# Front of a six-layer transformer kernel on one core: five small inputs moved to ScalarE's queue, context sums on two engines, value products issued later, products nobody reads put into waits

## The reference, cut to what matters

```python
x = x + L0_xattn(layernorm(x), ctx)     # x @ W1.T + mean over the 1601 context rows @ W2.T + b
x = x + L0_attn(layernorm(x))           # 16 heads of 16, scores + slopes[h] * (k - q), softmax
x = x + L0_ffn(layernorm(x))            # routed experts and a shared gated MLP (sw1, sw3, sw2)
x = x + L1_xattn(layernorm(x), ctx)     # 16 heads over 1601 keys and values made from ctx
x = x + L1_attn(layernorm(x))           # causal convolution, gated recurrence, gated MLP
x = x + L1_ffn(layernorm(x))            # 256 to 1024 to 256, quantized
```

## Time and profile before

| what | us |
|---|---|
| median of 3 runs | 2172.41 (2168.35 to 2173.95) |
| the profiled execution's own time | 2174.97 |
| its span in the profile | 2173.2 |
| TensorE busy | 1977.2 (91% of the span) |
| VectorE, ScalarE, GpSimd busy | 1328.9, 1049.6, 613.0 |

### The profile page before, as it was taken

One profiled execution on the slowest core, in us unless ns is written; L12 is line 12 of the kernel. 1 busy time (PEld: TensorE's weight loads), 2 busy tenths in 40 slices (PEclk: granted clock), 3 DMA queues, 4 the chain that ended last, 5 costly groups with the idle time before them and its releaser, 6 DMA issues.

```text
span 2173.2 us, 72578 instructions
## 1 busy us (share of the span) xinstructions
PE 1977.2 (91%) x31813; PEld 1596.8 (73%) x31813; DVE 1328.9 (61%) x2495; ACT 1049.6 (48%) x1534; POOL 613.0 (28%) x998
## 2 busy tenths in 40 slices
PE   4788989999999999999999999999999988999887
PEld 4567777777877777777777777777777777777764
DVE  2456755856666567656656676665666666565534
ACT  2344545554455555545555555554544444434432
POOL 3222332323233232333323223332323222122201
PEclk8899999999999999999999999999999999999999
DMA  4343423433423343334233424243342321222122
GB/s 160 140 150 109 142 87 125 149 125 124 139 88 114 116 141 129 130 107 151 83 125 109 171 77 138 92 150 106 110 148 89 116 79 31 89 83 81 48 66 72
DMA packets 99255, 243.91 MB, mean 112 GB/s; under 512 B 13312, under 2 KB 19584, under 8 KB 98944
## 3 DMA queue, kind: packets, MB, share of 16 engines
q1 hardware_dynamic: 98944, 239.26, 32.5%
HBM read 235.94 MB, written 3.15 MB: 110 GB/s over the span
## 4 chain that ended last, share of the span: by engine, by line
PE 71%; DVE 14%; ACT 9%; issue 4%; SPq 1%; POOL 1%; DMA 1%; DVEq 0%; POOLq 0%; ACTq 0%
PE M L780 12%; PE SC L977 9%; PE M L787 9%; PE SC L1000 8%; PE O L1021 7%; ACT probT L1220 6%; PE X L827 5%; DVE mx L1559 4%; PE SC L993 3%; PE M L827 3%; PE X L1101 2%; PE M L868 2%; DVE oT L1571 1%; PE X L1088 1%; PE M L832 1%
## 5 line engine op out<-in xcount | busy, mean ns | idle before, releaser
L1559 DVE TENSOR_REDUCE mx<-SC 128x4 f32<-128x1600 f32 (+1 forms) x256 | 466.5, 1822 | 131.4 <-PE SC L977 128.2
L1220 ACT ACTIVATE probT<-SC 128x2048 f32<-128x2048 f32 (+1 forms) x256 | 398.8, 1558 | 227.2 <-PE SC L1000 226.5
L634 POOL TENSOR_TENSOR rowsT<-raw,rowsT 128x384 fp32r<-128x384 f32 (+1 forms) x256 | 277.8, 1106 | 405.0 <-ACT rowsT L1278 404.9
L787 PE MATMUL M<-wvs,rowsT 128*128 128x256 f32 x2496 | 358.3, 292 | 3.2 <-issue 1.6
L780 PE MATMUL M<-rowsT,wks 128*128 128x400 f32 (+1 forms) x1536 | 334.5, 363 | 12.0 <-DVE V L1362 7.6
L780 PEld LDWEIGHTS M<-rowsT,wks 128*128 128x128 f32 x1536 | 276.2, 192 | 84.5 <-issue 61.5
L1362 DVE TENSOR_TENSOR V<-M,bv 128x256 f32<-128x256 f32 (+1 forms) x448 | 159.6, 398 | 287.4 <-PE M L787 276.6
L787 PEld LDWEIGHTS M<-wvs,rowsT 128*128 128x128 f32 x2496 | 314.8, 192 | 23.5 <-issue 3.5
L1165 ACT ACTIVATE kT<-M,bk 128x400 f32<-128x400 f32 (+1 forms) x256 | 151.6, 594 | 350.6 <-PE M L780 350.2
L977 PE MATMUL SC<-kT,bdq 32*128 32x400 f32 (+1 forms) x2048 | 248.1, 553 | 49.9 <-ACT probT L1220 42.7
L1021 PEld LDWEIGHTS O<-probT,V 128*17 128x17 f32 x13312 | 191.3, 98 | 72.2 <-issue 66.6
(11 more groups left out here) (266 smaller groups left out, 2464.1 us busy)
## 6 DMA issues: line engine op xcount, KB each, us to landing
ring<-in_ws_dram SPq DMA_DIRECT2D x428, 256.0 KB, 4.5
raw<-in_ctx_dram SPq DMA_DIRECT2D x32, 1601.0 KB, 8.4
summed<-in_ctx_dram SPq DMA_DIRECT2D x60, 800.5 KB, 4.5
ring<-rounded_scratch SPq DMA_DIRECT2D x64, 256.0 KB, 5.4
out_dram<-x SPq DMA_DIRECT2D x16, 128.0 KB, 3.2
kT<-in_ctx_dram SPq DMA_DIRECT2D x2, 800.5 KB, 8.9
x<-in_x_dram SPq DMA_DIRECT2D x11, 128.0 KB, 2.0
rounded_scratch<-wround SPq DMA_DIRECT2D x8, 128.0 KB, 2.2
```

The lines of the kernel that those rows point to most:

```text
L634: pool.tensor_tensor(rowsT[1][:, c, at], raw[:, c, at], rowsT[0][:, c, at], ALU.subtract).then_inc(low_ready, 1)
L787: mm = pe.matmul(bank[:, (t - 2 * a) * D:(t - 2 * a + 1) * D], rowsT[xp][:, cc, t * P:(t + 1) * P], wvs[wp][:, cc, :], start=(at == cc == ...
L1220: act.activation(probT[step % 3][0:w, :, 0:len(ts), :].rearrange("p j t q -> p j (t q)"), SC[0:w, :, 0:len(ts) * P], ACT.Exp)\
L1559: dve.tensor_reduce(mx[c][:, :, n], SC[:, :, 0:KCH[n][1]], AX.X, ALU.max).then_inc(max_used, 1)
```

## The change

- SP's list: wk and wv come right after the weight ring, on a semaphore of their own (wkv_in); bv0, bo0 and wg follow alone on early_in; bq0, bk0, dist and the two slopes go to ACT's queue, issued first of all there (prep_in). ACT also loads its table for Exp at the start.
- DVE runs prepare() at g = -21, ahead of the sum of raw, and adds up the second half of batch 1's context (kT[1]) itself; ACT adds up the first half only, and does so after its drain of turn1.
- High parts 0 and 1 move to g = -24 on ACT, parts 2 and 3 to -19 and -18; POOL's low parts go to -18, -18, -16 and -13. The weights' high parts go to the end of g = -19 and the low ones to -18. POOL's clear() goes to the first cycle.
- EARLY: the first six key pieces are at -17, -16 and -15, two values at -12, a key at -9 and -8, and a value in each cycle from -7 to -3.
- warm(16) ahead of the first xa, and warm(2) ahead of four of the first maxima steps: products of 512 columns into bank X which nobody reads.
- At the end: IDLE of xq is 15 in place of 5, and busy_rows goes.

The diff, with its unchanged lines cut:

```diff
@@ -92,7 +92,7 @@
-IDLE = {'sums': 2, 'out': 9, 'conv_in': 4, 'pw': 10, 'gru_in': 7, 'hg0': 2, 'hg1': 3, 'gow': 10, 'ff_in': 7, 'ff0': 2, 'fow': 0, 'xq': 5, 'up0': 0, 'hq': 14, 'down': 4}
+IDLE = {'sums': 2, 'out': 9, 'conv_in': 4, 'pw': 10, 'gru_in': 7, 'hg0': 2, 'hg1': 3, 'gow': 10, 'ff_in': 7, 'ff0': 2, 'fow': 0, 'xq': 15, 'up0': 0, 'hq': 14, 'down': 4}
@@ -146,9 +146,12 @@
-EARLY = {-16: [key(0, 0), key(0, 1)], -15: [key(0, 2), key(0, 3)], -14: [value(0), value(1), value(2)], -13: [value(3), value(4)], -12: [value(5)], -11: [key(1, 0)], -10: [key(1, 1)], -9: [key(1, 2)], -8: [key(1, 3)], -3: [value(6)]}
+EARLY = {-17: [key(0, 0), key(0, 1)], -16: [key(1, 0), key(1, 1)], -15: [key(0, 2), key(1, 2)], -12: [value(0), value(1)], -9: [key(0, 3)], -8: [key(1, 3)], -7: [value(2)], -6: [value(3)], -5: [value(4)], -4: [value(5)], -3: [value(6)]}
+
+FIRST_WARM = (1, 2, 3, 4)
 OWN = value(4), value(5), value(6)
-FIRST_SPLITS = (-19, -18, -17, -16)
+
+FIRST_SPLITS = (-24, -24, -19, -18), (-18, -18, -16, -13)
@@ -304,7 +307,7 @@
     yield n + 1, piece
-if g == FIRST_SPLITS[piece]:
+if STEPS * b + k == FIRST_SPLITS[late][piece]:
@@ -468,6 +471,7 @@
                         "O0_ready", "th0_ready", "first_kept", "l0_done"))
+wkv_in, prep_in = sp.sem("wkv_in"), sp.sem("prep_in")
@@ -552,19 +556,13 @@
     issued += 1
-for t, src in ((bv0, d["l0bv"].partition_broadcast(P)), (bo0, d["l0bo"].partition_broadcast(P)), (wg, d["l0wg"]),
-               (bq0, d["l0bq"]), (bk0, d["l0bk"]), (dist, d["dist"])):
+for t, src in ((wk, d["wkv"][:, 0, :, :]), (wv, d["wkv"][:, 1, :, :])):
+    sync.dma_start(t, src).then_inc(wkv_in, 16)
+for t, src in ((bv0, d["l0bv"].partition_broadcast(P)), (bo0, d["l0bo"].partition_broadcast(P)), (wg, d["l0wg"])):
     whole(t, src, early_in)
-head_pairs = d["slopes"].rearrange("(j a) -> a j", a=2)
-for n in range(2):
-    sync.dma_start(slopes[n * S:(n + 1) * S, :], head_pairs[n].partition_broadcast(S),
-                   allow_slow_non_contiguous=True).then_inc(early_in, 16)
-for t, src in ((wk, d["wkv"][:, 0, :, :]), (wv, d["wkv"][:, 1, :, :])):
-    sync.dma_start(t, src).then_inc(in_, 16)
-for t, src in ((bk, d["l1bk"]), (perm, d["perm"]), (bq, d["l1bq"])):
+sync.dma_start(bvv[:, :, :].rearrange("p h f -> p (h f)"), d["l1bv"].partition_broadcast(P)).then_inc(in_, 16)
+for t, src in ((bk, d["l1bk"]), (bq, d["l1bq"]), (bo, d["l1bo"].partition_broadcast(P)), (perm, d["perm"])):
     whole(t, src, in_)
-sync.dma_start(bvv[:, :, :].rearrange("p h f -> p (h f)"), d["l1bv"].partition_broadcast(P)).then_inc(in_, 16)
-whole(bo, d["l1bo"].partition_broadcast(P), in_)
@@ -730,14 +728,14 @@
     split_max(b + 1, 0)
-if g == L0_START[0] + 5:
+if g == L0_START[0] + 4:
...
     if t == 0 and k == 0:
-        pool.wait_ge(in_, 112)
+        pool.wait_ge(in_, 80)
@@ -747,9 +745,9 @@
     if (i, q) == (0, 3):
-        pool.wait_ge(early_in, 128)
+        pool.wait_ge(early_in, 48)
     layer0(i, q)
-if g == L0_START[0] + 1:
+if g == FIRST_CYCLE:
@@ -833,6 +831,9 @@
 def layer0(what, i, kind, f, bank):
+    if (i, kind) == (0, "l0_xa"):
+        pe.wait_ge(cleared, 1)
+        warm(16)
@@ -904,7 +905,7 @@
 if i == 0:
-    pe.wait_ge(early_in, 128)
+    pe.wait_ge(early_in, 48)
@@ -959,12 +960,20 @@
+                def warm(count):
+
+                    for _ in range(count):
+                        pe.matmul(X.rearrange("p (a t) -> p a t", a=4), identb[:, :], identb[:, :].unsqueeze(1).to_broadcast([P, 4, P]),
+                                  start=True, stop=True, skip_group_check=True)
...
                     k0, kn = KCH[n]
+                    if s in FIRST_WARM:
+                        warm(2)
@@ -1036,23 +1045,11 @@
-                def busy_rows(columns_):
-
-                    for wp, xp in PARTS:
-                        for j in range(4):
-                            r = slice(32 * j, 32 * j + 32)
-                            pe.matmul(SC[:, j, 0:columns_], rowsT[wp][r, 0, 0:P], rowsT[xp][r, 1, 0:columns_], start=True, stop=True, skip_group_check=True)
...
                         busy(IDLE.get(kind, 0))
-                        if kind == "xq":
-                            busy_rows(400)
-                            busy_rows(400)
-                            busy_rows(128)
-                            busy_rows(128)
@@ -1115,10 +1112,6 @@
 for b, k in SLOTS:
-    if STEPS * b + k == min(EARLY):
-        pe.wait_ge(in_, 112)
-        pe.wait_ge(cleared, 1)
-        pe.wait_ge(split_ready, 2)
@@ -1136,6 +1129,8 @@
     fill_x(what, b)
+if STEPS * b + k == min(EARLY):
+    pe.wait_ge(split_ready, 2)
@@ -1143,6 +1138,14 @@
+
+                for t, src in ((bq0, d["l0bq"]), (bk0, d["l0bk"]), (dist, d["dist"])):
+                    act.dma_start(full(t), src).then_inc(prep_in, 16)
+                head_pairs = d["slopes"].rearrange("(j a) -> a j", a=2)
+                for n in range(2):
+                    act.dma_start(slopes[n * S:(n + 1) * S, :], head_pairs[n].partition_broadcast(S),
+                                  allow_slow_non_contiguous=True).then_inc(prep_in, 16)
+                act.preload_act_table(ACT.Exp)
@@ -1162,6 +1165,8 @@
 k0, kn = KCH[a]
+if what == (0, *key(0, 0)):
+    act.wait_ge(in_, 80)
@@ -1278,7 +1283,7 @@
 def high_weights():
-    act.wait_ge(in_, 112)
+    act.wait_ge(wkv_in, 32)
@@ -1290,7 +1295,9 @@
                         src = summed[:, :]
-                    act.activation(src, src, ACT.Copy, accum_out=msum[:, j % 2, c:c + 1]).then_inc(sum_added, 1)
+
+                    if (j, c) != (1, 1):
+                        act.activation(src, src, ACT.Copy, accum_out=msum[:, j % 2, c:c + 1]).then_inc(sum_added, 1)
@@ -1307,8 +1314,6 @@
 load_table(b, k, ACT.Gelu)
-if STEPS * b + k == L0_START[0] + 5:
-    high_weights()
@@ -1323,12 +1328,18 @@
 for j, c in sums(b, k):
-    context_sum(j, c)
+    if j > 1:
+        context_sum(j, c)
...
         drain(what)
+for j, c in sums(b, k):
+    if j == 1:
+        context_sum(j, c)
+if STEPS * b + k == L0_START[0] + 3:
+    high_weights()
@@ -1355,6 +1366,8 @@
 m = min(2 * a + 2, KT) - 2 * a
+if what == (0, *value(0)):
+    dve.wait_ge(in_, 80)
@@ -1398,6 +1411,8 @@
 wait_filled(dve, what)
+if i == 0:
+    dve.wait_ge(early_in, 48)
@@ -1717,7 +1732,7 @@
 def prepare():
-    dve.wait_ge(early_in, 128)
+    dve.wait_ge(prep_in, 80)
@@ -1731,7 +1746,7 @@
 def clear():
-    dve.wait_ge(in_, 112)
+    dve.wait_ge(in_, 80)
@@ -1744,10 +1759,11 @@
 if (i, q) == (0, 1):
+    prepare()
...
     dve.tensor_reduce(msum[:, 0, :], raw[:, :, 0:KEYS], AX.X, ALU.add).then_inc(fast_sum, 1)
-if (i, q) == (0, 3):
-    prepare()
+    dve.wait_ge(batch_landed, 32)
+    dve.tensor_reduce(msum[:, 1, 1:2], kT[1][:, 0:KEYS], AX.X, ALU.add).then_inc(sum_added, 1)
```

## The result

| | before | after |
|---|---|---|
| median, 11 runs each on one chip | 2173.95 (2168.35 to 2180.63) | 2185.26 (2179.32 to 2204.4) |
| ratio, with its 95% interval | | 1.0062 (1.0038 to 1.0087) |
| the profiled execution's own time | 2174.97 | 2184.64 |
| its span | 2173.2 | 2182.8 |
| TensorE busy | 1977.2 | 1977.6 |

The change is slower by over 0.3%. The profiled pair is 9.7 us apart, and it splits so: 1.8 us of it lie ahead of the first exponential of the batches, 7.8 lie between the first and the last of their 256 exponentials, and none behind. (The last row is worked out from the starts of the exponentials of the scores, L1225 in after and L1220 in before, as the traces have them.) TensorE is busy for the same time in both: what was lost is idle time.

A forecast was written before the change was run, and what follows sets the result against it. TensorE, busy 1733 of 1850 us at 2.4 GHz from 200 to 2050, was taken as the bound, so only front and end could move: +1.2 + 1.8 - 3.9 + 1.1 - 1.2 = -1.0 us off 2172.41, 2171.4, range 2161 to 2181.

The forecast's parts named there:

- the side that had 0.21: Chance given to slower by over 0.3%: 0.18 for late slopes, 0.03 for pt0 to sw2 giving nothing with late slopes.
- 1, xa: Front, up to the first xa: DVE does prepare and two sums after the slopes land; start at 22.7, 4.6 us later.
- T: Time when the last of the two slopes' transfers lands, on ACT's queue: taken as 13.0 us, ends 11.5 and 22.
- 2, xa to strips: Front, first xa to the strips: qk's drain no longer waits for prepare, 3.4 us less, 13.6 in place of 17.0.
- 3, strips to pt0: Front, strips to pt0: four keys now stand on PE ahead of ACT's exponential; 17.1 us, 1.8 more.
- 4, pt0 to sw2: Front, pt0 to sw2: value pieces and keys leave PE, at most 8.4 us won; 3.9 less taken, ends 0 and 8.4.
- 5, sw2 to the first maxima: Front, sw2 to the first maxima step: a value piece now stands on PE before the first queries' product; 1.1 us more.
- 6, maxima steps, and on to the first exponential: Six maxima steps: value pieces keep PE busy, three steps run at the higher clock; 1.2 us less.
- 7, the end: Kernel's end: 15 unread products finish about when the old ones did and the last xq waits for DVE; nothing either way.
- any change between 200 and 2050 us: Listed sign that the prediction is wrong: the long middle stretch, taken as unchanged, moves at all.
- third rival: Front: slopes share the engines with big transfers and land near 20; with 22, xa 9 us later, 2180.4 us; chance 0.18.
- second rival: Maxima steps and first scores: value pieces and unread products hold 2.4 GHz there; 2165 us; chance 0.14.

The follow-up runs named there:

- e5: The kernel before with 12 small unread float products (48 TensorE instructions) in the wait for the first xa: 2189.40 us, ratio 1.0080.
- e3: The changed kernel with prepare() on DVE put back behind the sums, at step q = 3: 2180.62 us, ratio 1.0017 to the kernel before.
- e7: The changed kernel without the 24 unread products of its front: 2179.62 us, ratio 1.0028 to the kernel before.
- e12: e10 with the EARLY table of the kernel before (values ahead, last two keys late): 2169.70 us, one run.
- e15: e5 with the raw context of batch b+2 asked for at k = 6 instead of k = 5: 2182.94 us, ratio 1.0029 to the kernel before.
- e6: The changed kernel with 52 small unread float products (208 instructions) behind its 16: 2179.15 us, ratio 1.0010 to the kernel before.
- e4: The changed kernel with 104 small unread float products (416 instructions) behind its 16: 2171.52 us, ratio 0.9975 to the kernel before.
- e13: e5 with the raw context of batch b+2 asked for at k = 7 instead of k = 5: 2236.02 us, ratio 1.0267 to the kernel before.
- e16: e10 with the raw context of batch b+2 asked for at k = 6 instead of k = 5: 2156.40 us, ratio 0.9910 to the kernel before.
- e9: The changed kernel with the slopes loaded as one transfer, 64 contiguous bytes per partition, on the same queue: 2181.31 us, ratio 1.0017 to the kernel before.
- e10: e9 with 8 in place of 16 unread products and 88 small ones behind them: 2160.01 us, ratio 0.9922 to the kernel before.

## Why the prediction was wrong

It said 2171.4 (2161 to 2181), likeliest no change; it came out 13.9 us above that, outside the range, on the side that had 0.21. (9.7 of it are what the profiled pair is apart, 1.0 is the gain that was forecast; the rest is in the medians.) By its own parts (measured: differences of the starts in the timelines shown):

| part | forecast | measured | |
|---|---|---|---|
| 1, xa | +4.6 | +12.6 | T = 13.0 was 23.6 |
| 2, xa to strips | -3.4 | -3.4 | right: 13.6 us |
| 3, strips to pt0 | +1.8 | +0.5 | 15.7 us where 17.1 was forecast |
| 4, pt0 to sw2 | -3.9 | -3.5 | right: 17.1 us |
| 5, sw2 to the first maxima | +1.1 | +0.5 | 8.2 us where 8.7 was forecast |
| 6, maxima steps, and on to the first exponential | -1.2 | -4.9 | 22.5 us where it was 27.4 |
| 7, the end | 0 | 0 | right |
| the batches | 0 | +7.8 | the step that failed |

**"From 200 to 2050 us ... nothing in that part is changed; so the time can move only in the front and at the very end".** This is the step that failed. The code of the batches was unchanged, but not its place in the blocks of 256, and e5 shows that 48 instructions cost 13.3 us there with the front untouched. The row that could have raised it stood on the page (q8, 256 packets of 16 KB), and so did 6.7 us of "issue" at L1021. The text itself named "any change between 200 and 2050 us" as what would prove it wrong, and gave it no chance. The unread products, which were costed at nothing, carry the cost: the 24 of them are 48 instructions.

**T, the landing of the slopes**, was mis-sized by 10.6 us. By the prediction's own sum that alone made 2182.0, already outside the range. It priced 1024 packets at 108 a us from 3.5 us on, with nothing else going on; in fact they started at 6.9 us and, with q1 on the same engines at 88%, went at some 65 a us until 23.2. The three inputs ahead, 384 packets, had no part in the rate: the last of them started at 4.1 us. The third rival ("Slopes behind the big transfers") had the mechanism, with T near 20; its bound of 22 was too low. Its other half, that raw and kT come up to 2 us later, is borne out: kT took 10.2 us to land for 8.9, and in e3 the sum of raw starts at 9.66 for 8.85. The ring was slowed more (17.5 us to landing for 11.7), which the prediction did not have. The Trainium skill's rule ("DMA: Bandwidth & Descriptors", section "Queues, rings and completion order"), that an engine goes round robin between its rows a packet at a time, is borne out in kind: 399 packets of q10 went between 558 of q1. They were not one for one, though, and what the Trainium skill calls a packet there can hold many descriptors, which the trace's packets don't tell, so the rule gives no rate here.

Two smaller sizes. Prepare took 1.2 us in after (23.59 to 24.78), not the 3.9 of before, which gave 2.7 back in part 1; no run shows why it took longer in before. And the second rival, "The clock stays up", came true by half: 1.00 for 0.71 through the maxima steps, but 0.72 from 107 to 125 us. The scores start at 106.35 for 103.07, so the maxima steps themselves gave 3.4 us (its end was 4) and the first scores 1.5, together 3.7 more than forecast in part 6. Value pieces and unread products each hold the clock without the other (e7, e12), so the eight unread products, which the prediction priced at 1.1, bought nothing. Without the batches the errors of the front nearly cancel: +1.8 where -1.0 was forecast, 2.8 us apart. That would have been no change, as forecast, but by luck: T was 10.6 us off one way, and prepare and the clock 6.4 the other.

What stays open: why before's own stalls stand where they do at k = 3 (the excess there is 10.1 us in e5 and 8.6 in e15), what parts e6 and e7, and whether another shift beats 207; only 0, 47, 48, 96, 207 and 255 were tried.

## What to carry to other kernels

Instructions are data, and they come over the same DMA engines as the tensors: adding or removing a few products ahead of a long body moves every block's end in it, and here that alone was worth from +13 us (e5) to some -4 (the batches of e4, 2005.6 for 2010.0). So before an edit in the front is judged, run it at two or three paddings of unread products, and look at the first and the last instruction of the body apart; a stall with the releaser "issue" that cuts a group of small products in two is the sign. Where big loads are asked for matters as well: one cycle later gave e15 12.8 us in its batches, two cycles later cost e13 far more, and at the better shift one cycle gave nothing that stands out of the noise (e16). And inputs in single floats should be made contiguous before they are moved to another queue: on their own queue they were slow, and they slowed the others.

## What was not expected of the hardware

- TensorE's instructions come 256 at a time over q8; it stops at 449 + 256n until the nth packet is in, and goes on some 2.5 us after that packet's start (18 profiles).
- Twelve unread products of 16 columns cost 13 us in a kernel of 2174 us (e5), and 160 more instructions gained 21 (e9 and e10).
- A stall of 2.2 to 2.9 us costs more than itself: behind it the granted clock was 0.83 and 0.91 (after) or 0.81 and 0.94 (e5) in the two stretches of 20 us from 640 us, 1.00 where there was no stall.
- Two queues at once: 39 KB in 1488 packets on q10 took the ring's loads on q1 from 11.7 to 17.5 us to landing; 43 KB in 576 packets left them at 11.8 (e9). It is the packets that cost, not the bytes.
